# Second attention of a fused adaLN block: fp32 scores of two heads at once on quarter rows of the array, the rotation partner by DMA, batches unrolled and overlapped

## The reference, cut to what matters

```python
q, k, v = proj(Wq), proj(Wk), proj(Wv)
q, k = _rope(q, k, ...)              # x * cos + rotate_half(x) * sin
scores = einsum('bhqd,bhkd->bhqk', q, k) / sqrt(d); causal
tmp_attn = softmax(scores)
tmp_sum = sum(tmp_attn, axis=-2)     # column sums, per head
topk_idx = top_k(tmp_sum, 25)        # heavy columns
mask = heavy columns | band of 25 around the diagonal
probs = softmax(where(mask, scores, neg))
attn = einsum('bhqk,bhkd->bhqd', probs, v)
return attn @ Wo.T                   # added to x
```

## Time and profile before

| | |
|---|---|
| median of three runs | 2241.44 us (2241.01 to 2247.59) |
| profiled execution, its own time | 2239.64 us |
| its span (first to last instruction) | 2237.8 us |
| second attention in it | from 47.6 to 720.0 us |
| PE, DVE, ACT, POOL busy, share of the span | 91%, 59%, 42%, 10% |
| mean granted TensorE clock | 0.947 of 2.4 GHz |

### The profile page before, as it was taken

How to read it: one execution, slowest core, us unless ns; L and a number is a source line. 1 busy time by engine, 2 the same in 40 slices (tenths; PEclk the granted TensorE clock), 3 DMA queues, 4 the chain that set the end, 5 groups by cost and what they waited for, 6 DMA issues and landing times.

```text
span 2237.8 us, 86088 instructions
## 1 busy us (share of the span) xinstructions
PE 2033.8 (91%) x34733; PEld 1748.2 (78%) x34733; DVE 1325.7 (59%) x4942; ACT 950.0 (42%) x3354; POOL 230.7 (10%) x346
## 2 busy tenths in 40 slices
PE   5889999999996889766999999998999989999999
PEld 3677677767665768666898998898998988988987
DVE  3565575575565079555666666665666656666653
ACT  1355364464453212233444444443444444444432
POOL 0011011011102100000011010110110110111012
PEclk9999999999997999865899999999999999999999
DMA  6000000000000832200000000000000000000000
GB/s 249 1 1 0 0 0 0 0 0 0 0 1 32 291 113 73 67 17 3 18 17 18 13 18 18 27 4 19 27 4 28 18 19 13 18 18 13 4 12 10
DMA packets 53629, 66.07 MB, mean 30 GB/s; under 512 B 4384, under 2 KB 45792, under 8 KB 52416
## 3 DMA queue, kind: packets, MB, share of 16 engines
q1 hardware_dynamic: 50832, 46.48, 6.2%
q0 software_dynamic: 2448, 14.68, 2.0%
HBM read 44.34 MB, written 16.81 MB: 27 GB/s over the span
## 4 chain that ended last, share of the span: by engine, by line
PE 51%; DVE 4%; issue 2%; ACT 1%; DMA 0%; DVEq 0%; POOL 0%; ACTq 0%
PE ps L1302 27%; PE ps L1256 11%; PE ps L1236 11%; PE ps L1290 2%; PE ps L1245 1%; DVE hbuf L1472 1%; DVE dh L1460 0%; DVE dh L1466 0%; DVE hbuf L1469 0%; DVE cn L1450 0%; DVE ns L1462 0%; DVE h L1470 0%; ACT nn L1369 0%; DVE s L1438 0%; DVE cn L1438 0%
## 5 line engine op out<-in xcount | busy, mean ns | idle before, releaser
L1302 PE MATMUL ps<-hbuf,whf 128*128 128x32 f16 x24480 | 659.1, 178 | 82.9 <-DVE hbuf L1472 59.9
L1302 PEld LDWEIGHTS ps<-hbuf,whf 128*128 128x128 f16 x24480 | 648.3, 97 | 106.0 <-DVE hbuf L1472 60.4
L1349 ACT ACTIVATE rz<-s,sc 128x32 f32<-128x32 f32 x512 | 164.5, 321 | 524.1 <-DVE s L1438 512.6
L1236 PE MATMUL ps<-hbuf,w1f 128*128 128x256 f16 x2304 | 294.4, 275 | 0.0
L1256 PE MATMUL ps<-hh,w2f 128*128 128x256 f16 x2304 | 294.1, 276 | 0.0
L1438 DVE TENSOR_REDUCE s<-ps 128x32 f32<-128x64 f32 x512 | 114.5, 224 | 272.7 <-PE ps L1302 259.4
L1425 POOL TENSOR_TENSOR hh<-tb,hh 128x256 f16<-128x256 f32 x192 | 132.3, 694 | 1307.2 <-ACT hh L1396 1307.2
L1236 PEld LDWEIGHTS ps<-hbuf,w1f 128*128 128x128 f16 x2304 | 224.5, 98 | 33.3 <-issue 6.0
L1256 PEld LDWEIGHTS ps<-hh,w2f 128*128 128x128 f16 x2304 | 212.0, 98 | 45.9 <-issue 19.6
L946 PE MATMUL ps<-x1T,wi 128*128 x768 | 173.7, 389 | 21.2 <-DMA wi<-in_W_ih 12.6
L946 PEld LDWEIGHTS ps<-x1T,wi 128*128 128x128 f32 x768 | 149.1, 195 | 45.4 <-issue 19.6
(11 more groups left out here) (198 smaller groups left out, 2876.3 us busy)
## 6 DMA issues: line engine op xcount, KB each, us to landing
gi_d<-stage SPq DMA_DIRECT2D x96, 128.0 KB, 1.7
gi<-gi_d SPq DMA_DIRECT2D x16, 768.0 KB, 5.5
w1f<-in_w1T POOLq DMA_DIRECT2D x4, 1408.0 KB, 9.2
xall<-in_x SPq DMA_DIRECT2D x4, 1024.0 KB, 9.0
x1T<-in_xT SPq DMA_DIRECT2D x1, 4096.0 KB, 21.7
w2f<-in_w2T POOLq DMA_DIRECT2D x2, 2048.0 KB, 11.0
out<-x1T SPq DMA_DIRECT2D x8, 512.0 KB, 3.1
wi<-in_W_ih SPq DMA_DIRECT2D x1, 3072.0 KB, 10.5
```

Of the source, the lines that this page charges most:

```text
L1236: last = nc.tensor.matmul(ps[:, 6 + i % 2, 0:TT], w[:, wp, e % EH, c * P:(c + 1) * P], hbuf[par][:, k, hq, :, :].rearrange("p s b -> p (s ...
L1302: last = nc.tensor.matmul(ps[:, bank, g * WIDE * 2 * B:(g + 1) * WIDE * 2 * B], whp[:, k, w, q, g * P:(g + 1) * P], h[:, k, :, :].unsqueez ...
L1349: nc.scalar.activation(rz[:, q, :, :].rearrange("p g b -> p (g b)"), s1[:, q, :, :].rearrange("p g b -> p (g b)"), ACT.Sigmoid, scale=sc[: ...
```

## The change

1. Raw q and k stay in `raw`, doubled over batches, and are rotated in place. `rot`, `kz`, `tmp` and `hb` go, and with them the POOL copy and the four masked key copies. The scores of heads h and h + 1 are issued together: their masks first, then both 128-column matmuls, then both 256-column ones, each with 32 rows at `tile_position=(rows.start, 0)`, in different banks. Both heads' `p_s` increments come at the end.
2. The projections are cut into four units of 512 columns (q and k, each in two halves). The partner rows of a unit come from eight DMAs, SBUF to SBUF, 16 partitions of 2 KB each, issued by SP into `swp`, instead of the permutation matmuls. DVE rotates a unit in three steps of 512 columns.
3. No hardware loop: all eight batches are written out. Projections of the next batch, copies and rotation steps are placed at numbered slots (one slot is one head of a round; slots 16 and up are the second round), and the turning, attending, output projection (`close`) and addition of batch b move into the rounds of batch b + 1. `wv` and the last two `close` stand beside the top-25 search.

The diff, cut to its core (in order: the swap on SP; the scores and the two rounds on PE; one rotation step and the first round on DVE; the constants):

```diff
+                def swap(b, u):
+                    i, p = UNITS[u]
+                    sp.wait_ge(a_raw, b * NU + u + 1)
+                    passed(sp, v_rot, (b * NU + u - 1) * 3)
+                    x = raw[:, b % 2, i, 2 * p:2 * p + 2, :]
+                    half = DH2 // 2
+                    for to in range(0, P, half):
+                        of = to + half if to % DH2 == 0 else to - half
+                        sp.dma_start(swp[to:to + half, u % 2, :, :], x[of:of + half, :, :])\
+                            .then_inc(d_swap[u % 2], 16)
...
                 def scores(b, r, h):
+                    passed(pe, a_e, (n + 1 - 4 + 1) * 2)
+                    if r == 0 and h % (NH // 2) == 0:
+                        pe.wait_ge(v_rot, (b * NU + 2 + h // (NH // 4)) * 3)
+                    pair = [(g, g % 4, g // HPC, slice(g % HPC * DH2, (g % HPC + 1) * DH2)) for g in (h, h + 1)]
...
-                    nc.tensor.matmul(ps[:, bank, 0:P], rot[:, 0, m, 0:P], kz[:, q, m, 0:P],
-                                     start=False, stop=True, skip_group_check=True)
-                    nc.tensor.matmul(ps[:, bank, P:P + S], rot[:, 0, m, P:S], kz[:, q, m, :],
-                                     start=False, stop=True, skip_group_check=True).then_inc(p_s, 1)
+                    for g, bank, m, rows in pair:
+                        nc.tensor.matmul(ps[:, bank, 0:P], q_[rows, m, 0:P], k_[rows, m, 0:P], start=False, stop=True,
+                                         tile_position=(rows.start, 0), skip_group_check=True)
+                    for g, bank, m, rows in pair:
+                        nc.tensor.matmul(ps[:, bank, P:P + S], q_[rows, m, P:S], k_[rows, m, :], start=False,
+                                         stop=True, tile_position=(rows.start, 0), skip_group_check=True)\
+                            .then_inc(p_s, 1)
...
+                for b in range(B):
+                    for h in range(NH):
+                        if h % 2 == 0:
                             scores(b, 0, h)
+                        if b and h < AHEAD:
+                            turn(b - 1, NH - AHEAD + h)
+                        if b and h == AHEAD:
+                            attend(b - 1, KD - 1)
+                        side(b, h)
+                        if b and h in CLOSE_AT:
+                            close(b - 1, CLOSE_AT.index(h), 5)
+                        if h >= AHEAD_SUMS and (h - AHEAD_SUMS) % CGS == CGS - 1:
+                            column_sums(b, (h - AHEAD_SUMS) // CGS)
+                    values(b, 0)
+                    column_sums(b, NH // CGS - 1)
+                    values(b, 1)
+                    if b:
+                        pe.wait_ge(v_x, (b - 1) * KD + 2)
+                        close(b - 1, 2, 5)
+                        close(b - 1, 3, 5)
+                    pe.wait_ge(v_k, (b + 1) * K_STEPS)
...
+                    for h in range(NH):
+                        if h % 2 == 0:
+                            scores(b, 1, h)
+                        if h >= AHEAD:
+                            turn(b, h - AHEAD)
+                        side(b, NH + h)
...
+                    if step == 0:
+                        dve.wait_ge(d_swap[u % 2], (b * 2 + u // 2 + 1) * 8 * 16)
+                        nc.vector.tensor_tensor(y, y, sin, ALU.mult).then_inc(v_rot, 1)
+                    if step == 1:
+                        nc.vector.tensor_tensor(x, x, cos, ALU.mult).then_inc(v_rot, 1)
+                    if step == 2:
+                        dve.wait_ge(v_rot, n + 2)
+                        nc.vector.tensor_tensor(x, x, y, ALU.add).then_inc(v_rot, 1)
...
+                    for h in range(NH):
+                        maxima(b, 0, h)
+                        if h == 0:
+                            if b:
+                                normalise(b - 1, NH - 1)
+                        else:
+                            for_sums(b, h - 1)
+                        side(b, h)
...
+UNITS = ((0, 0), (1, 0), (0, 1), (1, 1))
+UNIT_BANK = (6, 6, 7, 7)
+PROJECT_AT = (0, 1, 3, 4, 7, 9, NH + 2, NH + 4)
+RAW_AT = (2, 5, 10, NH + 5)
+ROTATE_AT = (4, 5, 6, 7, 8, 9, 12, 13, 14, NH + 8, NH + 9, NH + 10)
+CLOSE_AT = (12, 13)
-NDG = 3
+NDG = 6
```

More of the change, by code:

```diff
@@ L40 @@
 C_ALL = C_DESC8 + NE
-C_ROT = 0
-C_CAUS = C_ROT + P
+C_CAUS = 0
 C_NB0 = C_CAUS + P
@@ L410, in second_attention, with passed, _ @@
         v_x = sem(st, "v_x")
+        def passed(engine, semaphore, value):
+            if value > 0:
+                engine.wait_ge(semaphore, value)
         with nc.Block() as block:
+            @block.sync
+            def _(sp):
+                def swap(b, u):
[9 more added lines that the diff above has]
+                for b in range(B):
+                    for u in range(NU):
+                        swap(b, u)
             @block.gpsimd
@@ new lines, in project @@
+                def project(b, u, part, bank):
+                    i, p = UNITS[u]
+                    w = (wq, wk)[i]
+                    m = 2 * p + part
+                    for k in range(KD):
+                        last = nc.tensor.matmul(ps[:, bank, part * S:(part + 1) * S], w[:, k, m * P:(m + 1) * P],
+                                                hT[:, k, b, :], start=(k == 0 and part == 0), stop=(k == KD - 1),
+                                                skip_group_check=True)
+                    if part == 1:
+                        last.then_inc(p_qk, 1)
@@ new lines, in close @@
+                def close(b, m, bank):
+                    pe.wait_ge(a_o, (b + 1) * KD)
+                    o = ps[:, bank, (m % 2) * S:(m % 2 + 1) * S]
+                    for k in range(KD):
+                        last = nc.tensor.matmul(o, wo[:, k, m * P:(m + 1) * P], oT[:, k, :],
+                                                start=(k == 0 and m % 2 == 0), stop=(k == KD - 1),
+                                                skip_group_check=True)
+                    last.then_inc(p_o, 1)
@@ L579, in _ @@
-                project(0)
-                for i in range(2):
-                    swap(0, i)
-                with pe.Fori(0, B - 1) as b:
-                    batch(b, True)
-                batch(B - 1, False)
+                            attend(b, g // HPC)
+                for g in range(NH - AHEAD, NH):
+                    turn(B - 1, g)
+                attend(B - 1, KD - 1)
+                for m in range(KD):
+                    close(B - 1, m, 2 * (m // 2))
             @block.scalar
@@ L644, in batch @@
[L644 to L650 removed]
+                        if b and h < 2:
+                            turned(b - 1, NH - 2 + h)
+                        if b and h == AHEAD + 1:
+                            attended(b - 1, KD - 1)
@@ new lines, in _ @@
+                        side(b, h)
+                    for c in range(KS):
+                        act.wait_ge(p_v, b * KS + c + 1)
+                        nc.scalar.activation(v[:, c, :], ps[:, 6 + c, :], ACT.Copy).then_inc(a_v, 1)
+                    for h in range(NH):
+                        exps(b, 1, h)
+                        side(b, NH + h)
+                        if h >= 2:
+                            turned(b, h - 2)
+                        if h >= 7 and h % HPC == 3:
+                            attended(b, (h - 7) // HPC)
@@ L652, in _ @@
+                for g in range(NH - 2, NH):
+                    turned(B - 1, g)
+                attended(B - 1, KD - 1)
             @block.vector
```

387 lines of the change are left out of this document (162 added, 225 removed).

## The result

| | before | changed |
|---|---|---|
| median | 2241.8 us (2238.5 to 2249.9, 14 runs) | 2259.5 us (2249.7 to 2271.4, 14 runs) |
| ratio | | 1.0084, interval 1.0065 to 1.0104 |
| profiled execution, span | 2239.6, 2237.8 | 2258.6, 2256.7 |
| second attention | 47.6 to 720.0 | 47.6 to 743.7 |

The changed kernel is 0.84% slower; 2174 us (3% faster) was forecast. The stage that was to end at 653.3 ends at 743.7.

The account below looks back on a forecast made before the run. PE was taken to bound the kernel, busy 75.8 of 81.4 us a batch. The second attention would end at 70.3 + 72 + 6 x 74 + 67 = 653.3 instead of 720.0, 66.7 less, giving 2174 us; range 2115 to 2222.

Parts of the forecast that it names:

- the price of the swap: Each unit's eight SP-issued DMAs: 4.6 us from ACT's raw copy to DVE's first rotation step, ends 3.5 and 9.
- I add 1.5: Second attention, each batch: 1.5 us added for TensorE's clock falling in PE's new waits, giving 74 us a batch.
- the walk: One batch of the second attention followed from its first pair at the estimated prices: period 72.5 us before the clock term.
- PE's work: PE's busy time in a new batch: first round 26.9, middle 11.9, second round 21.4, sum 60.2 us.
- The rival of the other side: Swap takes much longer, delaying DVE three to four times a batch; slower from a swap of about 7.7 us; chance 0.07.
- The rival "row tiles give little": Score pairs: weight loads serial or nothing side by side; 76 to 80 us a batch, 2190 to 2220; chance 0.2.
- The rival "swaps hidden": Swaps land in 3.5 us or slots run slower, so DVE never waits long; 66 a batch, 2116 to 2118; chance 0.25.
- the products of a pair: PE's score matmuls for two heads, run side by side on row tiles: 0.86 us for both, masks not included.
- the middle: Between the two rounds of a batch: search beside PE work 7.1 us, then light columns, hand-over and second diagonal 2.4.
- the four waits: DVE's idle time before each unit's first rotation step, waiting for the swap: about 0.8, 2.8, 3.9 and 0.5 us.
- The second round: Second scoring round of a batch: PE, DVE and ACT all at 21 to 22 us, taken as 23.5 with the first head's ramp.
- the likeliest case: The batch walk holds: 2145 to 2195 us, period 70 to 77 us; chance 0.45.

Follow-up runs that it names:

- kernel 4: The changed kernel with each of a unit's eight swap DMAs cut into two of half the columns, sixteen issues: 2436.1 us (one run).
- kernel 9: The changed kernel, slots unchanged, with four of the eight swap DMAs of units 0 to 2 issued by POOL instead of SP: 2200.7 us, 0.9819.
- kernel 1: The changed kernel without the swap's DMAs; DVE multiplies a partner tile of zeros and waits only for the raw copy: 2148.1 us, 0.9586.
- kernel 12: Kernel 8 with both heads of each pair on the 32 rows of the first head: 2258.4 us, 1.0074.
- kernel 13: Kernel 8 with score products on all 128 rows, without tile_position, pairs kept: 2188.5 us, 0.9760.
- kernel 14: The changed kernel at its own rotation slots, with score products on all 128 rows: 2251.5 us, 1.0042.
- kernel 8: The changed kernel with DVE's rotation steps at later slots, swap DMAs unchanged: 2172.5 us, 0.9694.
- kernel 5: The kernel before with only the quarter-row score pairs, plus three unused full-row bf16 matmuls of 512 columns after each first-round pair: 2296.6 us, 1.0234.

## Why the prediction was wrong

- **The first step that failed** is the price of the swap: "SP issues one each 8.42 - 8.06 = 0.36 us, the last after 2.6, and one lands 1.7 us after its issue: 4.6 us". The row came from stores of another kind; SP's next issues in the same trace, loads, stood 0.41 and 0.47 apart. The issues take 0.62 each here and the swap 6.3 us, within the bounds given (3.5 to 9). DVE's waits are 14.0 us a batch instead of 8.0. Kernels 4, 9 and 1 move this one cost up, down and away and the time goes with it, by 0.9 to 1.1 us for each us waited.
- **The step that put the time outside the range** is the next one, the term "I add 1.5" for TensorE's clock. With the swap at its measured price the walk gives a period of about 80 (1.7 us more, three to four times a batch), and 1656 + 7 x 80 = 2216 still lies inside 2115 to 2222. Batches 1 to 6, split as in the table, take 63.6 us of work, 12.9 of idle time and 8.3 lost to the clock; the walk had 60.2, 12.3 and 1.5. So 6.8 of the 10.8 us a batch that were missed stand in the clock, 3.4 in PE's work and 0.6 in idle time. The forecast read the loss of clock as a toll of each wait. That it lasts through work on quarter rows (kernels 12 and 13, 14 and the changed one) no row of before could show, and no bound was kept for it. The two steps hang together: without the waits (kernel 1) the clock costs 11.4 us in the stage and not 73.5.
- **PE's work** was priced 3.4 us a batch too low. About 1.5 of them are the pairs, 1.17 and 1.51 us with their masks instead of 1.08 and 1.41; the rest was not taken apart. The 9.3 us that the scores were to save are 9.0 by the forecast's own prices (8 x 0.56 + 8 x 0.57); nothing else was worked out from them.
- **The rival of the other side** came true in its mechanism (the swap takes longer, and DVE holds ACT and PE behind it), at a smaller swap than its condition and with the clock beside it. Its chance, 0.07, was too small, because the price in the rival stood on the swap alone: it made the kernel slower from a swap of 7.7 us, and 6.3 were enough.
- **The rival "row tiles give little"** was wrong in its mechanism, and right in that little of what the tiles save arrives. Loads of different row groups don't queue: 0.85 a pair, not 1.12, and with its masks 1.18 in the first round (425.19 to 426.37), not 1.49. The Trainium skill ("TensorE: Matmul & The Clock Gate", LDWEIGHTS (loading the stationary operand)) says that a load for 32 rows takes as long as one for 128. The traces agree with that: the median load of the score products takes 184 to 187 ns on 32 rows (changed kernel) and 192 on 128 (kernel 13). What failed is the rival's other condition, that such loads come one after the other. But of the some 52 us of work that PE is spared only 16 reach the time where the swap is hidden (kernels 13 and 8), and none where it is not (14).
- **The rival "swaps hidden"** was priced at 2116 to 2118 us. With the swap left out it is 2148, and hidden by later slots 2172. Kernel 8's period of 71.5 us (mean of six, search to search) splits into 63.7 of work, 5.6 idle and 2.2 lost to the clock, where the rival's 66 has 60.2, 5.8 and nothing: the idle time is right, work and clock are missing.
- **Right:** the products of a pair (0.86 forecast, 0.85), a landing near 1.7 us (1.9), the middle (9.5 forecast, 8.4), the place and order of the four waits, and the gain of the overlap itself: on full rows with the swap out of the way it gives 2.4%.
- **The second round**, 23.5 forecast, is 29.2: unit 3's wait was forecast as 0.5 and is 1.9, and behind it PE runs at 0.59 to 0.84 for 6 us. Kernel 8's batch, 71.5 on average and 70.1 in the window shown, is within the 70 to 77 of the likeliest case.

The 14 timed executions say the same of the clock: the fastest, 2249.7 us, has a mean granted clock of 0.928 over the span, the two slowest, 2270.9 and 2271.4, have 0.912 and 0.917.

## What to carry to other kernels

Where small DMAs replace work on an engine, the number of issues on one queue can set when the data is complete (here 4.9 of 6.3 us); put the consumer so late that the upper bound of the price is covered, not the value taken. A wait placed in an engine's own order can cost the whole kernel about its full length (0.9 to 1.1 us for each us here), part of it as a lower clock of TensorE. Time taken off TensorE counts only as far as its clock stays: split a stage into work, idle time and lost clock, in a kernel with the small tiles and in one without, before tiles are counted as a gain.

## What the hardware showed that was not expected

- SP needs 0.62 us for each issue of a DMA SBUF to SBUF of 16 partitions of 2 KB (4.94 for eight), POOL 0.48 to 0.50 (1.91 to 1.98 for four); one lands 1.9 us after its issue.
- Two fp32 heads on different row groups take 0.85 us, in either order of issue; on one row group 1.50; on full rows 1.37 to 1.46. With the masks in front it is 1.18 on quarter rows and 1.59 on full rows.
- Granted clock 0.50 for 13.0 and 15.7 us in which PE was busy all the time on quarter-row pairs, transposes and column sums, after waits of 3.40 us and of 1.28 us. With full rows in the same place of another batch it was 1.00 again about 5 us after a wait of 2.34 us. Over the stage PE worked 107 us at 0.50 in kernel 12 (32 rows, pair 1.50) and 14 us in kernel 13 (128 rows, pair 1.37), with ten waits above 1 us in each. Why it comes back in one and not in the other is open: more full-row matmuls between the pairs did not bring it back in each round (kernel 5).
